# One kernel, one table of orders: the last layer's second product moves from steps 0 and 1 to steps 6 to 9 of the middle batches

## The reference

```python
def attention(x):                      # 16 heads of 8
    q, k, v = split(x @ w_qkv)
    w = relu(q @ k.T / sqrt(8));  w = w / (sum(w) + 1e-6)
    y = x + (w @ v) @ w_out + b_out
    return layernorm(y) * gamma + beta

def ffn(x):                            # w1: 128 to 512, w2: 512 to 128, dequantised
    z = silu((layernorm(x) * g + be) @ w1 + b1) @ w2 + b2
    return x + 0.5 * z

x = x + 0.5 * ffn(layernorm(x))
x = x + attention(layernorm(x))
x = x + 0.5 * ffn(layernorm(x))
```

## Time and profile before

| | |
|---|---|
| median of 3 executions | 369.73 us (369.69 to 369.89) |
| span of the profiled execution | 369.5 us, 0.2 us under the median |
| TensorE busy | 360.0 us, 97% of the span |
| VectorE, ScalarE, GpSimd busy | 283.8, 231.4, 219.8 us |
| granted TensorE clock | 1.00 throughout, the 2.4 GHz level |
| chain that ended last | TensorE 87%, VectorE 4%, ScalarE, DMA, GpSimd 2% each |

### The profile page before, as it was taken

The page is one execution under the profiler, slowest core; times in us unless marked ns, Lnnn a source line. Parts: engine busy times, 40 slices in busy tenths (PEclk is TensorE's granted clock), DMA queues, the critical chain, the costliest instruction groups (busy, mean ns, idle before and its releaser), DMA issues.

```text
span 369.5 us, 11752 instructions
## 1 busy us (share of the span) xinstructions
PE 360.0 (97%) x4518; PEld 185.2 (50%) x4518; DVE 283.8 (77%) x689; ACT 231.4 (63%) x425; POOL 219.8 (59%) x447
## 2 busy tenths in 40 slices
PE   8999998999999999999999999999999999999996
PEld 8854433453564445653564434644456535532476
DVE  5876677897778977699777977689776797578774
ACT  3377465667847586466865678475864668588523
POOL 7595065547973589437992479635894377315541
PEclk9999999999999999999999999999999999999999
DMA  7016005500351005500173003610063001710001
GB/s 211 4 31 173 3 0 128 131 3 2 88 143 60 3 0 136 147 8 1 31 173 87 4 0 67 165 59 2 4 156 104 4 0 32 191 38 2 2 2 61
DMA packets 14103, 22.66 MB, mean 61 GB/s; under 512 B 2528, under 2 KB 3808, under 8 KB 14048
## 3 DMA queue, kind: packets, MB, share of 16 engines
q1 hardware_dynamic: 11456, 17.83, 20.1%
q10 hardware_dynamic: 2592, 4.07, 3.4%
HBM read 3.54 MB, written 2.10 MB: 15 GB/s over the span
## 4 chain that ended last, share of the span: by engine, by line
PE 87%; DVE 4%; ACT 2%; DMA 2%; issue 2%; POOL 2%; SPq 0%; POOLq 0%; DVEq 0%; ACTq 0%
PE o_bank L682 30%; PE scores L659 16%; PE pre_bank L603 9%; PE post_bank L603 9%; PE pre_bank L608 5%; PE pre_bank L609 3%; DMA q_op<-q_parts 2%; PE pre_bank L631 2%; PE post_bank L608 2%; PE pre_bank L596 1%; PE post_bank L609 1%; PE post_bank L631 1%; PE o_bank L590 1%; PE post_bank L596 1%; PE scores L608 1%
## 5 line engine op out<-in xcount | busy, mean ns | idle before, releaser
L1280 DVE TENSOR_SCALAR probs<-scores 128x512 f32<-128x512 f32 x242 | 155.8, 683 | 48.3 <-PE scores L659 45.0
L981 ACT ACTIVATE probs<-scores 128x512 f32<-128x512 f32 x262 | 141.7, 596 | 65.9 <-PE scores L659 65.9
L682 PE MATMUL o_bank<-probs,v_op 128*32 128x512 f32 x1024 | 135.9, 602 | 0.2
L659 PE MATMUL scores<-q_op,k_op 32*128 32x512 f32 x504 | 76.0, 494 | 1.9 <-DMA q_op<-q_parts 0.8
L659 PEld LDWEIGHTS scores<-q_op,k_op 32*128 32x128 f32 x504 | 31.9, 181 | 81.5 <-issue 54.4
L870 ACT ACTIVATE pre_y<-pre_bank,b_sum,col_consts 128x512 f32<-128x512 f32 x28 | 21.9, 782 | 23.6 <-PE pre_bank L631 23.5
L682 PEld LDWEIGHTS o_bank<-probs,v_op 128*32 128x32 f32 x1024 | 21.9, 108 | 28.4 <-issue 24.6
L603 PE MATMUL pre_bank<-w,pre_y 128*32 128x128 f32 x960 | 30.8, 274 | 0.0
L603 PEld LDWEIGHTS pre_bank<-w,pre_y 128*32 128x32 f32 x960 | 25.7, 110 | 8.1 <-issue 7.7
L603 PE MATMUL post_bank<-w,post_y 128*32 128x128 f32 x960 | 29.3, 273 | 0.0
L603 PEld LDWEIGHTS post_bank<-w,post_y 128*32 128x32 f32 x960 | 25.9, 110 | 5.6 <-issue 5.4
(11 more groups left out here) (219 smaller groups left out, 555.3 us busy)
## 6 DMA issues: line engine op xcount, KB each, us to landing
k_op<-k_parts SPq DMA_DIRECT2D x62, 128.0 KB, 2.7
q_op<-q_parts SPq DMA_DIRECT2D x62, 128.0 KB, 2.7
out_dram<-o_rows ACTq DMA_DIRECT2D x7, 256.0 KB, 2.0
pre_x<-in_x_dram ACTq DMA_DIRECT2D x6, 256.0 KB, 2.8
w_int<-in_L_ffn_fc_q_dram SPq DMA_DIRECT2D x2, 256.0 KB, 3.9
rows<-in_lines_dram ACTq DMA_DIRECT2D x1, 256.0 KB, 6.0
s_rows<-in_L_ffn_fc_scales_dram SPq DMA_DIRECT2D x1, 256.0 KB, 6.6
wqk<-in_w_qk_dram SPq DMA_DIRECT2D x1, 256.0 KB, 6.7
```

The costliest lines, as they stand in the source:

```text
L659: mm(score_bank(b, s, i, j), k_op[rows, g, P * kt:P * (kt + 1)], q_op[rows, g, :], start=True, stop=True).then_inc(scores_done[i], 1)
L682: last = mm(o_bank[pair][VW * j:VW * (j + 1), :], v_op[:, kt, heads_of(g).start + 2 * j, :], probs[:, s % 2, j, :], start=(odd == 0 and kt ...
L981: activation(probs[:, s % 2, 2 * i + j, :], score_bank(b, s, i, j), ACT.Relu).then_inc(probs_done[i][j], 1)
L1280: v.tensor_scalar(probs[:, s % 2, 2 * i + j, :], score_bank(b, s, i, j), 0.0, None, ALU.max).then_inc(probs_done[i][j], 1)
```

## The change

Most of it is in the tables. In batches 1 to 6 the four quarters of `post.fc2@-2` leave steps 0 and 1 and stand in steps 6, 7, 8 (late) and 9 (early); in batch 7 they go from steps 0 and 1 to steps 3 to 6. The pre layer's second product is drawn together in steps 4 and 5 (before: 4, 5 and 6). `uT`, `k`, `q` and `v` stand one step earlier, in 10 to 13; `post.hT` stands one step later, in 10; `post.fc1` stands in 11, 12, 13 and 14 instead of 11, 12, 13 and 15. `post.op` now comes ahead of the second product of the batch before it, so the two waits in the code below follow the bank's new order. ACT, DVE and POOL are moved to match: `out` to step 9 and the store to step 10, `x2_stats`, `x1`, `x1_stats`, `oT` and `den` to steps 5, 6, 7, 8 and 8, `post.hT` on DVE to step 11, `v_in.2` on POOL to the front.

```diff
 PE_ORDER = [
-    ([], ["post.fc2.0@-2", "pre.fc1.0@1"]),
+    ([], ["pre.fc1.0@1"]),
...
 DVE_ORDER = [
...
+    ["post.hT@-1", "pre.k_lo@1"],
...
                     if f == 0 and not (st is post and b == B - 2):
                         next_fill(st, b, "fc2")
+                        if st is post:
+
+                            pe.wait_ge(y_done, b + 2)
...
-                            pe.wait_ge(post.free, len(POST_FILLS) * b)
+                            pe.wait_ge(post.free, len(POST_FILLS) * (b - 1) + post.n("fc1.3"))
```

More of the change, by code:

```diff
@@ L71 @@
 PE_ORDER = [
-    ([], ["post.fc2.0@-2", "pre.fc1.0@1"]),
-    (["post.fc2.1@-2", "post.fc2.2@-2", "post.fc2.3@-2", "pre.fc1.1@1"], []),
+    ([], ["pre.fc1.0@1"]),
+    (["pre.fc1.1@1"], []),
     (["pre.fc1.2@1", "post.op@-1"], []),
     (["pre.fc1.3@1"], []),
-    (["pre.fc2.0@1"], []),
-    ([], ["pre.fc2.1@1"]),
+    (["pre.fc2.0@1"], ["pre.fc2.1@1"]),
     (["pre.fc2.2@1", "pre.fc2.3@1"], []),
[L79 to L87, removed]
+    ([], ["post.fc2.0@-2"]),
+    ([], ["post.fc2.1@-2"]),
+    ([], ["post.fc2.2@-2"]),
+    (["post.fc2.3@-2"], []),
+    (["pre.uT@1"], ["post.hT@-1"]),
+    ([], ["pre.k@1", "post.fc1.0@-1"]),
+    ([], ["pre.q@1", "post.fc1.1@-1"]),
+    ([], ["pre.v@1", "post.fc1.2@-1"]),
+    (["post.fc1.3@-1"], []),
+    (["pre.hT@2"], []),
 ]
@@ L92 @@
 PE_END = [
-    ([], ["post.fc2.0@-2"]),
-    (["post.fc2.1@-2", "post.fc2.2@-2", "post.fc2.3@-2"], []),
-    ([], ["post.op@-1"]),
     ([], []),
     ([], []),
-    ([], []),
-    ([], []),
+    ([], ["post.op@-1"]),
+    ([], ["post.fc2.0@-2"]),
+    ([], ["post.fc2.1@-2"]),
+    ([], ["post.fc2.2@-2"]),
+    (["post.fc2.3@-2"], []),
     ([], []),
@@ L144 @@
     ["pre.fc1.1@1"],
-    ["pre.fc1.2@1", "post.store@-2", "pre.load_x@2"],
+    ["pre.fc1.2@1", "pre.load_x@2"],
     ["pre.fc1.3@1"],
@@ L151 @@
     [],
-    ["post.hT@-1"],
     [],
[L154 to L158, removed]
+    ["post.store@-2", "pre.uT@1", "post.hT@-1"],
+    ["pre.k@1", "post.fc1.0@-1"],
+    ["pre.q@1", "post.fc1.1@-1"],
+    ["pre.v@1", "post.fc1.2@-1"],
+    ["post.fc1.3@-1"],
+    ["pre.hT@2"],
 ]
@@ L162 @@
     [],
-    ["post.store@-2"],
+    [],
     [],
@@ L167 @@
     ["post.y_apply@-1"],
-    [],
+    ["post.store@-2"],
     [],
@@ L207 @@
     ["oT.1@-1", "den.1@-1"],
-    ["a.1@-1", "post.out@-2", "aT@-1"],
+    ["a.1@-1", "aT@-1"],
     ["post.y@-1", "post.y_stats@-1"],
@@ L211 @@
     ["pre.x_stats@2"],
-    ["post.x2@-1"],
-    ["post.x2_stats@-1", "pre.x1@1"],
+    ["post.x2@-1", "post.x2_stats@-1"],
+    ["pre.x1@1"],
+    ["pre.x1_stats@1"],
+    ["oT.0", "den.0"],
+    ["post.out@-2"],
+    ["a.0"],
+    ["post.hT@-1", "pre.k_lo@1"],
+    ["pre.q_lo@1"],
     [],
-    ["pre.x1_stats@1"],
     [],
[L217 to L221, removed]
     ["pre.hT@2"],
@@ L225 @@
     [],
-    ["oT.1@-1", "den.1@-1", "a.1@-1", "post.out@-2", "aT@-1"],
+    ["oT.1@-1", "den.1@-1", "a.1@-1", "aT@-1"],
     ["post.y@-1"],
@@ L256 @@
 POOL_ORDER = [
-    [],
+    ["v_in.2"],
     ["post.u_bias"],
@@ L260 @@
     [],
-    ["v_in.2", "post.x2_stats@-1", "post.x_apply@-1", "pre.x1_stats@1"],
     [],
-    ["pre.u_apply@1"],
-    ["pre.x_stats@2", "pre.uT@1"],
-    [],
-    ["v_in.3", "pre.x_apply@2", "post.xr@-1"],
-    [],
+    ["pre.x_stats@2"],
+    ["post.x2_stats@-1", "post.x_apply@-1", "v_in.3"],
+    ["pre.x1_stats@1", "pre.u_apply@1"],
+    [],
+    ["pre.x_apply@2"],
+    ["pre.uT@1"],
+    ["post.xr@-1"],
+    ["pre.x1_beta@1"],
     ["v_in.0@1", "v_in.1@1"],
-    ["pre.x1_beta@1"],
-    [],
     ["pre.xr@2"],
```

## The result

The changed kernel is slower: 377.6 us (median of four executions, 376.2 to 378.8) against 369.81 us before, ratio 1.0204 (95% interval 1.0176 to 1.0232). The same kernel was run again beside the experiments: 376.65 against 370.19, 1.0185 (1.0164 to 1.0206). I had forecast 375.3 and a range of 371.0 to 379.0: the side and most of the mechanism held, the size came out too small. The profiled execution (376.2 us, span 374.4) carries the comparison.

A forecast was written before the change was run, and what follows sets the result against it. TensorE, busy 360.0 of 369.5 us, bounds the kernel. Differences made in the profiled execution, its span read as 0.2 under the median, were added: 369.73 + 2.5 (middle batches) + 3.05 (batch 1) = 375.3 us, range 371.0 to 379.0.

The forecast's parts named there:

- Steps 1 and 14: Waits behind ScalarE's silu for the bank: +0.50 in step 1 (batches 2 to 6) and in step 14 (batches 1 to 6).
- Step 11: `fc1.0` waits for VectorE's late low part and may start at 2.58: +0.34 in batches 1 to 6, bounds 0 to 0.5.
- the 0.3 that was named as a sign: Expected in the profile after: step 11 near 3.4 with about 0.3 of idle TensorE time ended by L1059.
- Stalls removed: In a middle batch the score waits of steps 8, 10 and 11 go, -1.09; that of step 4 stays.
- steps 6 to 9: In middle batches, one quarter each: 2.30 per step, over the 1.98 VectorE's relus need, with score rows of 0.50.
- load: TensorE's matmuls in a middle batch with changed neighbours: 42.0 against 41.73, +0.25, possibly 0 to 0.4.
- Batch 1: Four bare steps, 6 to 9, wait for VectorE: +3.05, from 39.89 to 42.9, bounds 2.0 to 3.8.
- the other terms, which were to cancel: In batch 1, beside its bare-step waits: 0.25 - 1.09 + 0.50 + 0.34, leaving 3.05 in all.
- Batch 7: Bare first steps and a waiting `op` against a part-covered normalisation and less idle time: -0.8 to +1.1, taken as 0.
- the idle time in step 8 that was to go: In batch 7, up to 0.61 of idle time was to go in step 8.
- `x2` held: Rival, 0.23: GpSimd's power holds VectorE's `x2` in step 5, which ends 0.4 later: +1.4, 376.7 us.
- The even load: Rival, 0.08: the three hand-overs cost nothing, a middle batch is 0.84 less than now: 365.5 us.

The follow-up runs named there:

- 4: Changed kernel with the first layer's quarters 1, 2 and 3 behind the value products of steps 1, 2 and 3, no longer ahead: 374.0 us.
- 2: Changed kernel with the last quarter of the last layer's first product behind the value products of step 14, in batches 1 to 6: 375.14 us.
- 1: Changed kernel with batch 1 alone keeping the old orders on all four engines: 373.64 us.
- 8: Changed kernel with 3.5 us of spare small matmuls in steps 6 to 9 of batch 1 alone: 377.23 us.
- experiment 10: Changed kernel with batches 6 and 7 keeping their old orders: 376.66 us.
- experiment 9: Changed kernel, batches 1 and 7 old, three hand-over waits of steps 1, 11, 14 undone, VectorE's division behind the relus of step 1: 367.07 us, 0.9918.

## Why the prediction was right or wrong

- *Steps 1 and 14:* right. +0.50 each was forecast, 2.83 for the step, with 0.4 to 0.5 idle behind the silu; 2.82 and 2.83 with 0.44 and 0.43 were measured, and experiments 4 and 2 gave back 0.50 and 0.51.
- *Step 11:* right mechanism, mis-sized term. Forecast +0.34, measured +0.44: the start at 2.58 was exact; that a broken run of matmuls loses 0.10 was left out. The idle time that the trace shows is 0.18 and not the 0.3 that was named as a sign, as the matmul ahead is drawn to its modelled end.
- *Stalls removed, steps 6 to 9, load:* right. The steps take 9.21 together (4 x 2.30); 0.56 - 0.50 - 0.50 - 0.44 + 1.09 leaves 0.21 for the load, taken at 0.25. Its sixteen fills are twelve quarters, `op`, `v` and the two last quarters; the "fifteen" of the text is a slip that the sum doesn't use.
- *Batch 1:* right. Forecast +3.05, measured +2.97, shown by experiments 1 and 8. The closeness is partly luck: the waits in steps 7 to 10 come to 2.77 instead of 3.05 by the step lengths, 0.18 of the difference in step 7, as `x2` took 0.68 and not 0.90; the other terms, which were to cancel, came to 0.20.
- *Batch 7:* wrong. This is the step that failed: "From -0.8 to +1.1; I take 0". The step lengths of batch 7 give +1.06, its upper end. Both costs stood in the text (bare first steps, `op` behind the division) and weren't followed step by step. Against the earlier trace rows, steps 0 to 6 went from 15.12 to 16.02: the first stalls by 0.54 (its scores 1.04 instead of 0.50), and step 2 takes 3.40 where a step with one fill takes 2.30, `op` idle for 0.45 of it; waits of 0.75 that steps 4 to 6 had before are gone. Steps 7 and 8 gave back only 0.30, and steps 9 to 14 took as much again, 10.58 instead of 10.27; the last 0.15 lies behind them and was not followed. So the idle time in step 8 that was to go gave back nothing in sum. The stall of the first step came out of batch 6, which the text had treated as a batch like the others (experiment 10).

```profile
320.70 1.04 PE L662 MATMUL scores<-q_op,k_op 32*128 32x512 f32 x4
...
326.50 1.08 PE L603 MATMUL post_bank<-wo,aT 128*32 128x128 f32 x32 [0.45 <-DVE aT L1084]
```

Steps 9 to 14 of batch 7, before:

```profile
335.67:345.94 10.27, 10.19 (x78) 3.01 (x75) 8.06 (x21) 7.77 (x16) 6.89 (x18) 1.00 0.01 2
```

and in the changed kernel:

```profile
340.37:350.95 10.58, 10.41 (x74) 3.00 (x74) 8.15 (x21) 8.25 (x17) 7.21 (x18) 1.00 0.05 19
```

- *The clock, and the rest:* the clock was not foreseen, about 1.5 us in some executions. By the step lengths the error is 6.44 - 5.55 = 0.9, batch 7's 1.06 less the small rest. The first median, 377.6, lies 2.3 above the forecast; it stands between two executions at a mean clock of 1.00, so what is left there, 1.4, isn't explained by the clock and stays open. The repeat, 376.65, leaves 0.45.
- *The rivals.* `x2` held fell: it runs in 0.68 beside the power (next section but one). `u` was never late: `uT` doesn't wait in step 10. The even load is real, but only once the hand-overs are gone: a middle batch of experiment 9 is at 42.12, and that case had worked out 42.2. In this change they ate it. The whole of experiment 9, 367.07, stays 1.6 above the 365.5 of that case.
- *The base.* Each later execution of the kernel before lies some 1.8 us above its span (369.72 at 367.9). By that the profiled execution of before, at a span of 369.5, was one of some 371.3 us (an estimate) and not 0.2 under the median, as the text reads it. That the span after is shorter "because its records begin later", as was expected ahead of the repeat, isn't borne out: its execution too lies 1.8 above its span. As the sum was made of differences, it isn't touched.

## What to carry to other kernels

When fills are evened out over a schedule, count for each what it waits for in its bank as well as what it takes: here 0.50 us behind a silu in two places and 0.44 behind a late low part ate a gain of 0.9 us per batch, and moving these fills to the other side of the value products, with one low part a step up, gave it back. Follow the batches at the ends, which share a table but lack some of its fills, step by step; a value between two bounds is no estimate. And once waits are taken out of one engine, look for the next that is late: in the middle batches the sum of single gains came true only when VectorE's order was mended too.
